# The last stage of an adaLN attention block, moved into the attention as one job per odd step

## The reference, cut to what matters

```python
# x: 4096 tokens x 256 channels; 16 heads of 16; mod = silu(c) @ wmod gives sa, ca, ga, sb, cb, gb
h = layernorm(x) * (1 + ca) + sa
q, k, v = split(h @ W_attn)
att = softmax(causal(q k^T / 4)) * decay(distance)     # decay is 0 from a distance of 512 on
x = x + ga * ((att @ v) @ W_proj)
h = layernorm(x) * (1 + cb) + sb
out = x + gb * (h @ (W + lilora)^T + b)
```

## Time and profile before

| | |
|---|---|
| time, three runs | 1557.61, 1557.8, 1559.09 us (median 1557.8) |
| the profiled execution | 1560.74 us, its span 1558.8 us |
| first scores of the attention | 205.9 us into the span |
| the attention's last instruction before `redo` is read | 1472.2 us |
| third stage | 1473.3 us to the end |
| busy | ACT 84%, PE 82%, DVE 64%, PEld 47%, POOL 3% |
| TensorE's granted clock, mean | 0.966 |
| q loads | 192 DMAs of 64 KB |

### The profile page before, as it was taken

The page is one execution under the profiler, slowest core; times in us unless marked ns, Lnnn a source line. Parts: engine busy times, 40 slices in busy tenths (PEclk is TensorE's granted clock), DMA queues, the critical chain, the costliest instruction groups (busy, mean ns, idle before and its releaser), DMA issues. The chain is left out here.

```text
span 1558.8 us, 28424 instructions
## 1 busy us (share of the span) xinstructions
PE 1280.6 (82%) x11067; PEld 737.5 (47%) x11067; DVE 996.6 (64%) x2026; ACT 1311.0 (84%) x2677; POOL 52.4 (3%) x28
## 2 busy tenths in 40 slices
PE   7876168888888888888888888888888888777598
PEld 5543034545454545444445444554544444333387
DVE  4632147777777777777777777777776666554376
ACT  2533069999999999999999999999999999999532
POOL 0322000000000000000000000000000000000022
PEclk9988579999999999999999999999999999999799
DMA  4999970101010101010100000000101000100153
GB/s 149 203 218 198 169 97 1 35 1 35 2 35 1 35 1 29 7 35 2 27 10 17 20 13 23 11 26 8 25 6 27 9 23 10 23 4 4 37 168 128
DMA packets 111723, 72.96 MB, mean 47 GB/s; under 512 B 56395, under 2 KB 110946, under 8 KB 111586
## 3 DMA queue, kind: packets, MB, share of 16 engines
q1 hardware_dynamic: 111586, 71.13, 21.3%
HBM read 45.93 MB, written 25.17 MB: 46 GB/s over the span
## 5 line engine op out<-in xcount | busy, mean ns | idle before, releaser
L808 PE MATMUL fast_s_ps<-k_stack,fast_q_stack 96*128 96x512 bf16 (+3 forms) x2448 | 651.9, 354 | 178.2 <-ACT fast_probs L927 98.7
L927 ACT ACTIVATE fast_s_ps<-fast_s_ps,fast_negmax 128x1024 f32<-128x1024 f32 (+4 forms) x768 | 792.8, 1039 | 4.4 <-PE fast_s_ps L808 3.9
L949 DVE TENSOR_REDUCE fast_negmax<-fast_s_ps 128x1 f32<-128x640 f32 (+4 forms) x512 | 399.1, 780 | 134.5 <-PE fast_s_ps L811 130.0
L927 ACT ACTIVATE fast_probs<-fast_s_ps,fast_negmax 128x640 f32<-128x640 f32 (+7 forms) x512 | 436.6, 853 | 43.3 <-DVE fast_negmax L949 38.7
L958 DVE TENSOR_TENSOR fast_probsT<-fast_t_ps,fast_dec_c 128x384 f32<-128x384 f32 (+2 forms) x512 | 276.6, 540 | 197.1 <-PE fast_t_ps L826 197.1
L808 PEld LDWEIGHTS fast_s_ps<-k_stack,fast_q_stack 96*128 96x128 bf16 x2448 | 180.0, 97 | 451.2 <-ACT fast_s_ps L927 178.0
L826 PE MATMUL fast_t_ps<-ident,fast_probs 128*128 128x128 f32 x1488 | 250.2, 275 | 22.7 <-DVE fast_y_sb L989 20.8
L968 DVE TENSOR_TENSOR fast_probsT<-fast_t_ps,fast_dec_c 128x256 f32<-128x256 f32 x464 | 191.6, 413 | 66.9 <-PE fast_t_ps L842 66.9
L826 PEld LDWEIGHTS fast_t_ps<-ident,fast_probs 128*128 128x128 f32 x1488 | 172.4, 141 | 76.2 <-DVE fast_y_sb L989 27.9
L842 PE MATMUL fast_t_ps<-ident,fast_probs 128*128 128x128 f32 x912 | 187.2, 286 | 1.9
L857 PE MATMUL fast_t_ps<-fast_probsT,fast_vals 128*16 128x128 f32 x4800 | 180.9, 276 | 7.1 <-DVE fast_probsT L968 5.9
(11 more groups left out here) (107 smaller groups left out, 588.1 us busy)
## 6 DMA issues: line engine op xcount, KB each, us to landing
parts_d<-part SPq DMA_DIRECT2D x48, 256.0 KB, 12.5
k_stack<-parts_d SPq DMA_DIRECT2D x48, 256.0 KB, 9.7
fast_q_stack<-parts_d SPq DMA_DIRECT2D x192, 64.0 KB, 3.0
fast_vals<-v_d SPq DMA_DIRECT2D x36, 128.0 KB, 3.0
xs<-x_dram SPq DMA_DIRECT2D x8, 512.0 KB, 8.6
v_d<-w SPq DMA_DIRECT2D x8, 512.0 KB, 8.6
y_d<-fast_y_sb SPq DMA_DIRECT2D x32, 128.0 KB, 2.5
yy<-y_d SPq DMA_DIRECT2D x16, 256.0 KB, 2.7
```

The source lines that it names most:

```text
L808: last = nc.tensor.matmul(s_ps[:, n % SLOTS, o:o + w], q, k_stack[:, h, P * b0 + o:P * b0 + o + w], start=True, stop=not diag)
L927: nc.scalar.activation(dst, src, ACT.Exp, bias=negmax[:, p % 2, side, h:h + 1], scale=-1.0, accum_out=sums[:, p % 2, side, h, c:c + 1]).th ...
L949: nc.vector.tensor_reduce(out=negmax[:, p % 2, side, h:h + 1], in_=s_ps[:, n % SLOTS, max(0, cols - P * WIN):cols], axis=AX_X, op=ALU.min) ...
```

## The change

The third stage is no longer run after `attention_fast`; its code is now `rest_full()` and runs only where `attention_full` does. In its place a finished pair's work is cut into jobs, one or two for an odd step of the next pair. Two tables name them:

```diff
+            HEAD_JOBS = {1: ("back", FAR), 3: ("back", NEAR), 13: ("n_turn", NEAR)}
+            TAIL_JOBS = {5: ("y_turn", NEAR), 7: ("project", FAR), 9: ("project", NEAR), 11: ("n_turn", FAR),
+                         13: ("linear", FAR), 15: ("linear", NEAR)}
...
             for s in range(NSTEP):
...
-                if back_after(s):
-                    next_turn("back", *back_after(s))
+                if job_after(s, HEAD_JOBS):
+                    next_turn(*job_after(s, HEAD_JOBS))
+                if job_after(s, TAIL_JOBS):
+                    next_tail(*job_after(s, TAIL_JOBS))
                 next_unit(FAR, s)
```

A head job uses the first bank and stands before `turn(FAR, s)`; a tail job uses the second and stands between `turn(FAR, s)` and the step's fifth piece, as a group's second part does in an even step:

```diff
                         fill(s, 3)
-                        if back_after(s):
-                            side, done = back_after(s)
-                            turn_back(done, side)
+                        if job_after(s, HEAD_JOBS):
+                            head_job(*job_after(s, HEAD_JOBS))
                         turn(FAR, s)
                         if group_after(s):
                             values(*group_after(s), 1)
+                            fill(s, 4)
+                            turn_tail(FAR, s)
+                        elif job_after(s, TAIL_JOBS):
+                            tail_job(*job_after(s, TAIL_JOBS))
                             fill(s, 4)
                             turn_tail(FAR, s)
                         else:
```

The jobs on TensorE: `y_turn` (four transposes), `project` and `linear` (two matmuls of 256 columns each), `n_turn` (two transposes). On VectorE, each frees the bank for the next use:

```diff
+                    def copy_y(p):
+                        dve.wait_ge(tail_full, tail_no["y_turn", NEAR, p] + 1)
+                        nc.vector.tensor_copy(tT[:], tail_ps.rearrange("p (s c q) -> p s c q", s=2, c=CH)).then_inc(tail_free, 1)
...
+                    def spread(side, p):
+                        dve.wait_ge(tail_free, tail_no["project", side, p] + 1)
+                        nc.vector.bn_stats(q6[:, side, :], xb[:, p % 2, side, :]).then_inc(raw_stats, 1)
...
+                    def result(side, p):
+                        dve.wait_ge(tail_full, tail_no["linear", side, p] + 1)
+                        dve.wait_ge(bias_added, 2 * p + side + 1)
+                        x2 = xb[:, p % 2, side, :]
+                        nc.vector.tensor_tensor(x2, x2, tail_ps[:, 0:C], ALU.add).then_inc(tail_free, 1)
...
+                    def row_sums(h, p):
+                        if h in (8, 10):
+                            spread((h - 8) // 2, p)
+                        if h in (9, 11):
+                            statistics((h - 9) // 2, p)
```

`residual` is as `result` with x, and `copy_n` copies 256 columns. GpSimd computes the inverse root by Newton steps, in eleven instructions on one element in each partition, each of which waits for the one before, then normalises and adds the bias:

```diff
+                    def inverse_root(side):
+                        v, half, y, w = (b[:, side:side + 1] for b in (var_e, var_h, rstd, root_t))
+                        chained(nc.gpsimd.tensor_scalar(v, mv2[:, side, 1:2], EPS, None, ALU.add))
+                        chained(nc.gpsimd.tensor_scalar(half, v, -0.5, None, ALU.mult))
+                        chained(nc.gpsimd.tensor_scalar(y.bitcast(mybir.dt.int32), v.bitcast(mybir.dt.int32),
+                                                        -0.5, 1597463007.0, ALU.mult, ALU.add))
+                        for _ in range(4):
+                            chained(nc.gpsimd.tensor_scalar(w, y, y, half, ALU.mult, ALU.mult))
+                            chained(nc.gpsimd.tensor_scalar(y, w, three_halves[:, 0:1], y, ALU.add, ALU.mult))
...
+                            nc.gpsimd.tensor_scalar(y_sb[:, side, :], x2, mv2[:, side, 0:1], rstd[:, side:side + 1],
+                                                    ALU.subtract, ALU.mult).then_inc(norm_ready, 1)
+                            pool.wait_ge(norm_ready, 2 * p + side + 1)
+                            nc.gpsimd.tensor_tensor(x2, x2, f_bias[:], ALU.add).then_inc(bias_added, 1)
```

SyncE loads q for half a pair at a time (`load_q(u)`: 12 DMAs of half the size, so that the buffer is half as large), loads x for a pair, and stores the result instead of y:

```diff
+                    for u in range(2 * NPAIR):
+                        p = u // 2
+                        if u + 2 < 2 * NPAIR:
+                            sp.wait_ge(s_full, PER * QH * (u + 1))
+                            load_q(u + 2)
...
+                        if u % 2 == 1 and p > 0:
+                            store(p - 1)
+                            if p + 1 < NPAIR:
+                                sp.wait_ge(result_stored[(p - 1) % 2], 32 * ((p - 1) // 2 + 1))
+                                load_x(p + 1)
```

More of the change, by code:

```diff
@@ L710, in attention_fast @@
                 next_tail("group", side, NSTEP // HG - 1)
-            for side in (FAR, NEAR):
-                next_turn("back", side, NPAIR - 1)
+            for kind, side in HEAD_JOBS.values():
+                next_turn(kind, side, NPAIR - 1)
+            for kind, side in TAIL_JOBS.values():
+                next_tail(kind, side, NPAIR - 1)
             s2 = ExitStack()
@@ L788, in _ @@
                     store(NPAIR - 1)
-                    for side in range(2):
-                        sp.wait_ge(y_stored[side], 16 * NPAIR)
+                    for b in range(2):
+                        sp.wait_ge(result_stored[b], 16 * NPAIR)
                 @block.tensor
@@ L869, in turn_back, with y_turn @@
                         last.then_inc(turn_full, 1)
+                    def y_turn(p):
+                        pe.wait_ge(tail_free, tail_no["y_turn", NEAR, p])
+                        pe.wait_ge(turn_free, turn_no["back", NEAR, p] + 1)
+                        for side in (FAR, NEAR):
+                            for cc in range(CH):
+                                o = P * (CH * side + cc)
+                                last = nc.tensor.transpose(tail_ps[:, o:o + P], y_sb[:, side, P * cc:P * (cc + 1)], ident[:])
+                        last.then_inc(tail_full, 1)
@@ L1660 @@
+            rest_full()
 def kernel(**inputs):
```

584 lines of the change are left out of this document (348 added, 236 removed).

## The result

| | before | after |
|---|---|---|
| median, us (runs) | 1558.4 (4) | 1544.6 (4) |
| lowest to highest, us | 1557.6 to 1568.1 | 1543.1 to 1548.1 |
| profiled execution: its time, its span | 1560.7, 1558.8 | 1545.3, 1542.7 |
| first exponential starts | 207.7 | 201.9 |
| last exponential starts | 1462.8 | 1506.3 |

The runs of before are those made beside the changed kernel. The ratio is 0.990, with an interval from 0.986 to 0.994. The change makes the kernel faster, by 14 us (0.9%) and not by 49; 1544.6 lies outside the range given. The span is 32.7 us longer than the sum of the prediction, and by its terms: the start 2.3 us better (5.8 won for 3.5), the attention from its first exponential to its last **49.4 us longer for 22** (+27.4), the stretch from the last exponential to the last `finish` 1.9 better (6.6 for 8.4), and the last pair **29.8 us for 20.3** (+9.5).

The account below looks back on a forecast made before the run. ScalarE was taken to set the attention's pace. Last `finish` 1471.2, less 3.5 for the start, plus 22 for jobs and 20.3 for the last pair, gave a 1510.0 us span, forecast 1509 us; range 1493 to 1537.

Parts of the forecast that it names:

- What the change removes: Third stage behind the last `finish` at 1471.20 goes, save the last pair's needs; half-size loads start the attention 3.5 us earlier.
- The matmuls themselves, about 0.6 us, are done beside the decay: Ordinary job in an odd step: its matmuls are hidden, so a narrow step pays nothing; 4.4 us for four kinds.
- The floor: Odd attention step without a job: 4.71 or 4.72 us, set by ScalarE's work on a pair's 33 blocks.
- A job has the wait of a group, but not its delay: Odd steps have no values ahead, so the chain to the next first exponential starts about 0.5 us earlier.
- rival 1: Attention's job steps: a job costs what a group does, 24 us inside, 1533 us in all; chance 0.18.
- Step 13: Attention step with a head job as well: 5.42 us when narrow, +0.71; taken as 13 us in all.
- Step 5: Attention step with `y_turn`, a 512-column copy of 0.69 us: narrow step 4.92, together 4.6 us.
- Row statistics and SyncE: Statistics in steps 8 and 10, and 12 more DMA issues a pair: nothing; without the statistics' cover 18 us.
- GpSimd's chain: Eleven small instructions at 0.3 us, then normalise and bias at 0.8 each; hidden in the attention up to 0.8 an instruction.
- rival 4: GpSimd too slow, TensorE waits at `n_turn` in steps 11 and 13: 1685 us at 1.27 an instruction; chance 0.05.
- Rival 3: GpSimd holds up VectorE's decays in the attention: +15 us, 1524 us in all; chance 0.10.
- The last pair: Behind the last `finish`, nothing hides its jobs: 20.3 us; 15.9 and 41.6 at 0.1 and 1.27 us a small GpSimd instruction.

Follow-up runs that it names:

- the one with ScalarE's root: Changed kernel, with the last pair's inverse root from a ScalarE square root and VectorE reciprocal, its normalisation on VectorE: 1534.5 us, ratio 0.983.

## Why the prediction was wrong in size and right in direction

- **What the change removes**: right. The third stage is gone from the path. The start gained 5.8 us for 3.5 in this execution; over the twelve profiles with the halved q the first exponential starts anywhere from 198.9 to 207.7, with a middle of 203.5, 4.2 earlier than before. The term is no better known than that.
- **The failing step is "The matmuls themselves, about 0.6 us, are done beside the decay".** A product takes 1.03 us and ends 0.31 after VectorE wants it. The evidence was at hand: the earlier trace rows have eight records of `at_ps` in 3.82 us, which the prediction took for eight matmuls of the code and which are four. So its "about 2.6" us of TensorE for a pair's jobs lacked half of four products: they alone are 4.1. The floor left a narrow step 0.19 us (4.71 - 4.52) before a job costs anything, and the job's operation started 0.39 later than priced. Steps 7, 9 and 15: 13.2 us for about 3. `n_turn` FAR, which has two transposes in place of the product, came out at nothing in the narrow steps, as predicted (4.71), and at 0.5 in all for 1.1.
- **"A job has the wait of a group, but not its delay"**: right for its own step; rival 1 had 5.1 for all job steps. But only the job's own step was looked at. The slack that it takes there was the lead of the even step behind it: 7.8 us, in no term.
- **Step 13**: 18.9 us without the dip, for 13. The 0.9 for `n_turn` NEAR was exact; the result of `linear` started 0.40 later behind its decay than priced, and 15 times that is the 6 us missing. **Step 5**: 2.6 for 4.6, on the safe side.
- **The clock**: 6.2 us of dips, in no term. The terms of the attention now add up: 9.9 for steps 7, 9 and 15, 5.9 for 13, 7.8 for the even steps, 6.2 for the clock, less 2.0 and 0.6 for steps 5 and 11, and 0.2 in pair 0 make 27.4 us.
- **Row statistics and SyncE**: nothing, as said.
- **GpSimd's chain**: hidden, as said. In the attention TensorE never waits for it:
```profile
L942 PE MATMUL fast_t_ps<-ident,fast_y_sb 128*128 128x128 f32 x56 | 10.7, 272 | 0.0
```
  so rival 4 is out. A small instruction is 0.34 us and 0.44 from start to start where it has two tensors for scalars, for 0.3 assumed, and the normalise 1.25 for 0.8: 5.8 us for a tile and not 4.1. Rival 3 is out as well, since the decays kept 540 and 413 to 415 ns; here the Trainium skill (SBUF — State Buffer, section "SBUF: two separate sides"), by which GpSimd shuts out only those operations of VectorE that run in a 2-port mode or read two SBUF inputs, agrees with the rows: the decays read one operand from PSUM and one from SBUF.
- **The last pair**: `y_turn`, the statistics and `n_turn` came as priced. Too small were `project` with its residual (2.6 for 1.5), GpSimd (12.4 for 9.0), the two results (4.4 for 2.6) and what lies behind the last result (6.6 for 3.4). The first and the third are the length of a product again, here at half the clock. The 6.6 stays unexplained.
- **The range** reached 1537 by rivals 1 to 3. The bound of +48 for the jobs stood in the text; with it alone the range would have ended near 1535, so what the range lacked was this term and the last pair's being off together. Of rival 4, the gain is gone at 0.91 us for a small instruction and not at 0.89, once the last pair is counted; nothing hangs on it, since 0.44 was measured.

## What to carry to other kernels

Count the records of an operation in the trace against the calls in the code before pricing it: an fp32 product of 256 columns is two. When work is slipped into a full pipeline, ask not only whether its engine has room but behind which wait its evacuation stands: in front of a wait that is there anyway it cost 0.0 us a step; one operation later, behind that wait, 0.2 to 0.3 us as a mean where its own producer was long, 0.03 where it was short, and 1.3 with two jobs in the step, and the next step lost up to 0.1 more. Moving the producer alone can be worse than not moving at all.

## What the runs showed of the hardware

- A product of two accumulating fp32 matmuls of 256 columns is four records. At the full clock (1.00 granted) it takes 1.03 to 1.13 us (379 ns a record, with their overlap), at half the clock (0.50) 1.92 to 2.08.
- GpSimd: a one-column operation with two tensor scalars 0.34 us, with constants 0.19 to 0.23, the next about 0.10 after either; a 128x256 operation with two tensor scalars 1.25 us, a sum of two tensors 0.72. VectorE does the 128x256 operation with two tensor scalars in 0.41.
- Three executions of kernels that differ in nothing in the attention (the changed kernel twice, the one with ScalarE's root) had their clock dips in steps 1, 3 and 13, of partly different pairs: 14 and 15; 6 and 14; 14 and 15.
